# Edge messages of a graph layer on one core: term rows in two float32r parts, and four selected columns instead of three in every other pair

## What is computed

```python
h = relu(layernorm(x))                         # x: 12500 nodes x 32
e_feat = concat([h[src], h[dst], edge_attr])   # 412500 edges, sorted by dst; 32 + 32 + 32 features
v = relu(e_feat @ W1 + b1) @ W2 + b2           # 96 -> 64 -> 32
x_cand = segment_max(v, dst, 12500)            # maximum over the edges of each destination node
out = x + maximum(x_cand, h)
```

## Time and profile before

| what | value |
|---|---|
| median of 3 runs | 3399.03 us (3394.15 to 3399.92) |
| profiled execution, its time | 3395.84 us |
| its span | 3394.0 us |
| PE busy, share of the span | 93% |
| DVE and POOL busy | 75% each |
| ACT (ScalarE) busy | 22% |
| selected columns, gathered columns | 604, 2620 |

### The profile page before, as it was taken

The page is one execution under the profiler, slowest core; times in us unless marked ns, Lnnn a source line. Parts: engine busy times, 40 slices in busy tenths (PEclk is TensorE's granted clock), DMA queues, the critical chain, the costliest instruction groups (busy, mean ns, idle before and its releaser), DMA issues.

```text
span 3394.0 us, 50502 instructions
## 1 busy us (share of the span) xinstructions
PE 3143.3 (93%) x14306; PEld 2377.7 (70%) x14306; DVE 2536.5 (75%) x4366; ACT 748.6 (22%) x1058; POOL 2533.3 (75%) x2651
## 2 busy tenths in 40 slices
PE   2699999999999999999999999999999999999996
PEld 1477777777777777676777777777776777777774
DVE  8387887887887777777777777776777777777776
ACT  5022222222222222222222222222222222222221
POOL 6777777777777777777777777777777777777774
PEclk9799999999999999999999999999999999999998
DMA  5623333333333333333333333333333333333331
GB/s 129 158 70 81 81 80 77 79 79 81 80 77 81 75 78 70 76 73 74 72 74 77 71 76 71 76 76 70 76 73 74 74 74 75 69 78 72 75 70 33
DMA packets 239673, 263.56 MB, mean 78 GB/s; under 512 B 80044, under 2 KB 193310, under 8 KB 233072
## 3 DMA queue, kind: packets, MB, share of 16 engines
q10 hardware_dynamic: 20790, 103.55, 12.3%
q1 hardware_dynamic: 134330, 115.08, 11.2%
q0 software_dynamic: 84352, 43.18, 10.5%
HBM read 250.01 MB, written 11.62 MB: 77 GB/s over the span
## 4 chain that ended last, share of the span: by engine, by line
POOL 46%; PE 29%; issue 15%; DVE 4%; DMA 3%; SPq 2%; POOLq 1%; DVEq 0%; ACT 0%
POOL feat L517 46%; PE ps_spare L608 16%; PE ps_hid L617 3%; PE ps_hid L619 3%; DMA feat<-h_rows,idx 2%; PE ps_picked L649 2%; PE ps_val L628 2%; PE ps_feat L575 1%; SPq L336 1%; PE ps_val L638 1%; DVE feat_t L919 1%; DVE sel_tmp L994 0%; POOLq L505 0%; SPq L303 0%; DVE best L1033 0%
## 5 line engine op out<-in xcount | busy, mean ns | idle before, releaser
L517 POOL DMA_INDIRECT feat<-h_rows,idx x2620 | 2516.5, 960 | 817.4 <-issue 790.2
L608 PE MATMUL ps_spare<-table,key_hot 128*128 128x448 f32 x8456 | 1942.7, 385 | 31.0 <-DVE key_hot L983 25.0
L608 PEld LDWEIGHTS ps_spare<-table,key_hot 128*128 128x128 f32 x8456 | 1616.0, 193 | 266.1 <-issue 127.6
L1033 DVE TENSOR_TENSOR best<-ps_picked,best 32x64 f32 x1612 | 356.1, 221 | 565.9 <-PE ps_picked L649 376.9
L983 DVE TENSOR_TENSOR key_hot<-key_ring,ps_iota 128x896 fp32r<-128x896 f32 x604 | 650.7, 1078 | 30.4 <-DMA key_ring<-key_rows 30.4
L617 PE MATMUL ps_hid<-feat_t,w_blk 128*128 128x512 f32 x806 | 432.7, 618 | 0.0
L994 DVE SCALAR_TENSOR_TENSOR sel_tmp<-off_place,offset,ps_spare 128x448 f32<-128x448 f32 x604 | 407.4, 675 | 12.3 <-PE ps_spare L608 9.3
L619 PE MATMUL ps_hid<-edge_hot,dst_rows 128*128 128x512 f32 x806 | 411.6, 592 | 0.0
L1001 DVE TENSOR_REDUCE feat<-sel_tmp 128x32 f32<-128x448 f32 x604 | 374.5, 620 | 20.8
L758 ACT ACTIVATE hidden<-ps_hid,b_col 128x1024 f32<-128x1024 f32 x202 | 225.4, 1116 | 606.3 <-PE ps_hid L619 606.3
L770 ACT CAST ends<-ps_val 128x512 fp32r<-128x512 f32 x202 | 118.2, 585 | 1020.7 <-PE ps_val L638 1015.7
(11 more groups left out here) (122 smaller groups left out, 770.8 us busy)
## 6 DMA issues: line engine op xcount, KB each, us to landing
dst_rows<-loc_rows ACTq DMA_DIRECT2D x98, 512.0 KB
feat_t<-attr_rows_in ACTq DMA_DIRECT2D x98, 512.0 KB
feat<-h_rows,idx POOLq DMA_INDIRECT x2620
key_ring<-key_rows SPq DMA_DIRECT2D x101, 384.0 KB, 3.4
dst_rows<-term_rows SPq DMA_DIRECT2D x404, 64.0 KB
dst_rows<-keep_rows SPq DMA_DIRECT2D x100, 256.0 KB
term_rows<-best SPq DMA_DIRECT2D x3, 1792.0 KB
idx<-src_cols_in SPq DMA_DIRECT2D x51, 32.0 KB
```

Source lines behind the costliest of these rows:

```text
L517: nc.gpsimd.indirect_dma_start(feat[:, slot, k, :], None, h_dram, bass.IndirectOffsetOnAxis(ap=idx[:, c % IDX, k:k + 1].bitcast(U32), axis=0),
L608: mm = pe.matmul(ps_sel[j % 2], key_hot[:, j % HOTS, g, :], table[half][:, g, :], start=(g == 0 and half == 0), stop=(g == SG - 1 and half ...
L1033: mm = nc.vector.tensor_tensor(col, ps_picked[D * q:D * q + D, to:to + WIN], col, ALU.max)
```

## The change

`SEL` becomes (4, 3): even pairs have 4 selected columns, odd pairs 3. A helper `columns(v)` gives the number of the first column of pair v. The term rows are split as the table already was: ScalarE rounds them into one float32r part, DVE subtracts for the second, and the first layer multiplies each by a one-hot that is now float32r too. `HOTS` goes from 4 to 2.

```diff
-SEL = 3
-HOTS = 4
+SEL = (4, 3)
+SPAN = len(SEL)
+HOTS = 2
...
+def columns(v):
+    return sum(SEL) * (v // SPAN) + sum(SEL[:v % SPAN])
...
-        edge_hot = sb("edge_hot", [P, 2, 4 * P])
+        edge_hot = sb("edge_hot", [P, 2, 4 * P], F32R)
+        term_half = [sb(f"term_half{n}", [P, 2, P], F32R) for n in range(2)]
...
-            sp.wait_ge(S["key_out"], 16 * NSB)
-            sp.wait_ge(S["off_step"], 5)
-            win_dmas(sp.dma_start, x, x_even, False, 0, T, S["x_win_in"])
...
+            sp.wait_ge(S["key_out"], 16 * NSB)
             for n in range(2):
-                load_key(2 * SEL * n, n)
+                load_key(columns(2 * n), n)
...
+            sp.wait_ge(S["sel_ready"], columns(NP - 1) + 1)
+            win_dmas(sp.dma_start, x, x_even, False, 0, T, S["x_win_in"])
             sp.wait_ge(S["best_done"], 1)
...
             def first_layer(i, v):
                 pe.wait_ge(S["edge_hot_ready"], i * UP + v + 1)
+                pe.wait_ge(S["term_split"], i * UP + v + 1)
...
-                    mm = pe.matmul(ps_hid[:, c, :], term_ring[:, slot, :], edge_hot[:, c, :],
-                                   start=False, stop=True, skip_group_check=True)
+                    for half in range(2):
+                        mm = pe.matmul(ps_hid[:, c, :], term_half[half][:, c, :], edge_hot[:, c, :],
+                                       start=False, stop=half == 1, skip_group_check=True)
...
             def step(i, v):
-                ahead = [j for j in range(SEL * v + 2 * SEL - 1, SEL * v + 3 * SEL - 1) if is_column(i, j)]
+                mid = [j for j in range(columns(v + 1) + 2, columns(v + 2)) if is_column(i, j)]
+                ahead = [j for j in range(columns(v + 2), columns(v + 2) + 2) if is_column(i, j)]
...
-                for j in ahead[0:1]:
+                for j in mid[0:1]:
                     select(i, j)
...
+                for j in mid[1:2]:
+                    select(i, j)
                 first_layer(i, v)
-                for j in ahead[1:3]:
+                for j in ahead:
                     select(i, j)
...
+            def round_terms(i, v):
+                n, slot = wide(i, v), TWO * v % RING
+                if v % 2 == 0:
+                    act.wait_ge(s_aux[v // 2 % 2], i * (2 * AUX) + (v // 4 * AUX + AUX))
+                nc.scalar.copy(term_half[0][:, 0:n, :], term_ring[:, slot:slot + n, :]).then_inc(S["term_hi_ready"], 1)
...
+            def split_terms(i, v):
+                n, slot = wide(i, v), TWO * v % RING
+                dve.wait_ge(S["term_hi_ready"], i * UP + v + 1)
+                nc.vector.tensor_tensor(term_half[1][:, 0:n, :], term_ring[:, slot:slot + n, :],
+                                        term_half[0][:, 0:n, :].bitcast(F32), ALU.subtract
+                                        ).then_inc(S["term_split"], 1)
...
                 place_edges(i, v)
+                split_terms(i, v)
                 for j in ahead[0:1]:
                     take_selected(i, j)
```

More of the change, by code:

```diff
@@ L103, in gnn_layer @@
         key_hot = sb("key_hot", [P, HOTS, SG, P], F32R)
-        key_ring = sb("key_ring", [P, 4 * SEL, P])
+        key_ring = sb("key_ring", [P, columns(4), P])
+        falls = sb("falls", [P, CE], BF16)
+        sel_tmp = sb("sel_tmp", [P, SN])
         offset = sb("offset", [P, NSEL])
-        sel_tmp = sb("sel_tmp", [P, SN])
         key_i = sb("key_i", [P, SG], I32)
@@ L254, in gathered @@
         def gathered(c):
-            return COLS - 1 - c % TWO
+            return COLS - (SEL[c // TWO % SPAN] + c % TWO) // TWO
         def is_column(i, j):
-            return not known(i) or j < SEL * (NP - 1) + 1
+            return not known(i) or j < columns(NP - 1) + 1
         def column(j):
-            n = j % SEL
-            return TWO * (j // SEL) + min(n, 1), COLS - 1 - n // 2
+            v = max(v for v in range(NP) if columns(v) <= j)
+            n = j - columns(v)
+            return TWO * v + (0, 1, 1, 0)[n], COLS - 1 - n // 2
         def load_rows(eng, s, half, count):
@@ L351, in load_key @@
             def load_key(s, half):
-                lo, n = half * 2 * SEL, 2 * SEL
+                lo, n = columns(2 * half), columns(2 * half + 2) - columns(2 * half)
                 sp.dma_start(key_ring[:, lo:lo + n, :].rearrange("p c e -> p (c e)"),
@@ L567, in turn_features @@
                 n = wide(i, v)
-                pe.wait_ge(S["sel_ready"], i * (SEL * UP) + (SEL * v + (SEL if n > 1 else 1)))
+                pe.wait_ge(S["sel_ready"], i * columns(UP) + (columns(v + 1) if n > 1 else columns(v) + 1))
                 for c in range(TWO * v, TWO * v + n):
@@ L675, in _ @@
             pe.wait_ge(S["table_ready"], 2)
-            for j in range(2 * SEL - 1):
+            for j in range(columns(1) + 2):
                 select(0, j)
@@ L1039, in step @@
             def step(i, v):
-                ahead = [j for j in range(SEL * v + SEL, SEL * v + 2 * SEL) if is_column(i, j)]
+                ahead = [j for j in range(columns(v + 1), columns(v + 2)) if is_column(i, j)]
                 if later(i, v - 1):
@@ L1052, in step @@
                     keep_best(i, v - 2)
-                for j in ahead[2:3]:
+                for j in ahead[2:]:
                     take_selected(i, j)
@@ L1070, in _ @@
                 place_keys(0, j)
-            for j in range(SEL):
+            for j in range(columns(1)):
                 take_selected(0, j)
@@ L1137 @@
     blocks = [np.asarray(src)[a:a + CE].reshape(2, P, Q)[1] for a in padded[0:len(begins) + len(begins) % 2]]
-    picked = np.stack([block[:, q] for n in range(0, len(blocks), 2)
-                       for block, q in ((blocks[n], Q - 1), (blocks[n + 1], Q - 1), (blocks[n + 1], Q - 2))])
+    picked = np.stack([blocks[TWO * v + (0, 1, 1, 0)[n]][:, Q - 1 - n // 2]
+                       for v in range(len(blocks) // TWO) for n in range(SEL[v % SPAN])])
     given["sel_rows"], given["sel_cols"] = picked, picked.T
```

37 lines of the change are left out of this document (18 added, 19 removed).

## The result

The changed kernel takes 3465.27 us (median of 4 runs, 3463.39 to 3466.4), against 3398.41 for the kernel before in the same series: ratio 1.02, 95% interval 1.0186 to 1.0213. Said was 3432. The direction was right, the size half of what came. The profiled execution took 3465.08, its span is 3463.2.

A forecast was written before the change was run, and what follows sets the result against it. Before, PE and later POOL's gathers bound it; after, a DVE-PE ring at 16.20 us per step. 197 x (16.20 - 15.96) = +47, start -9, end -5: +33 on 3395.84 gives 3429, median 3432; range 3355 to 3510.

The forecast's parts named there:

- The ring: In the loop, DVE and PE wait on each other through the one-hot; sets the step at 16.20 us, +47 in all.
- the end: The three steps behind the 200th: less term work and no gather wait, -5 us.
- the start: Before the third step: keys load earlier because x no longer loads ahead of them, -9 us.
- the walk of the ring: Sum of DVE and PE pieces from one pick_ends: 15.07 us with three takes, 17.32 with four, mean 16.20.
- Restart and select: In the loop, PE restarts after the one-hot, 0.28 us, then does the select's 14 matmuls, 2.82 us.
- steps of alternately about 14.4 and 18 us: Sign in the loop that would show the forecast right: step times alternating between these two lengths.
- PE's own work: PE's matmuls per loop step, without waits: 15.72 us, bounds 15.60 and 16.5.
- float32r term matmul: First-layer term matmul of 512 columns on PE: 0.235 us, bounds 0.206 and 0.43.
- The subtraction: New DVE instruction for the second term part, 256 elements, in the loop: 0.35 us, bounds 0.1 and 0.69.
- Rival 2: In place_edges on DVE, float32r one-hot loses double pace: step 16.66 us, total 3523; chance 0.14, shared with similarly large waits.
- the likeliest case: The loop's DVE and PE cycle as walked, with its bounds: 3406 to 3480 us, chance 0.56.
- The lesser form of rival 2: In the loop, POOL's gathers and the SBUF subtraction delay each other by 0.1 to 0.2: 3450 to 3470, counted with the forecast.

The follow-up runs named there:

- section 5: Series where the kernel before took 4373 to 4452 us instead of 3398: variants in buffers, take order, x load and columns, ratios to it 1.009 to 1.109.

## Why the prediction was right and where it was wrong

- **Who bounds.** Right. The ring closed, and four buffers, which open it and leave the rest, are 115 us faster.
- **The size.** Forecast +33, measured +69.2 us of span: the branch +53.4 that was not in the sum, the rest of the ring 24 us shorter than said, the end 5.4 and the start 1.1 us longer than said.
- **The step that failed** is the walk of the ring: "take 2.25 ... scan 1.13", and from it "Sum 15.07 ... Mean 16.20 us". It took DVE's time from one step in the middle of a turn and held it for all. Every eighth step has the branch between take and scan. The profile of before had the row for it: the scan's idle time, ended by "issue", 23 times. It belongs to the terms that a slack hides, and the change took the slack. It was put at nothing. Measured it is 34.5 us of idle time on DVE, 40 us in the steps and, with the lower clock behind nine of them, +53 us.
- **The rest of the ring** was 0.12 us too long per step (16.08 for 16.20), 24 us in all, which hid nearly half of the miss. Restart and select take 3.00 instead of 3.10, the three-take step 14.95 instead of 15.07; in the step with four takes, 17.20 for 17.32, PE's own 17.12 is as good as the bound. (The sign "steps of alternately about 14.4 and 18 us" does not follow from the prediction's own 15.07 and 17.32, and it was not seen.)
- **PE's own work** 15.675 (said 15.72), and the float32r term matmul at about 0.235 (0.233 from its start to the next matmul's): right. The subtraction 0.34 (said 0.35), `edge_hot` at its old pace:

```profile
L995 DVE TENSOR_SCALAR edge_hot<-dst_rows,place 128x1024 fp32r<-128x1024 bf16 x202 | 151.0, 747 | 4.7 <-DMA dst_rows<-term_rows 4.5
```

  Rival 2 falls with this row: 747 ns, 740 before. That was right for the reason given.
- **Start** -7.9 (said -9): right in size. The cause rests on when the keys were issued (section 5), not on a run with x alone moved in normal conditions.
- **End** +0.4 (said -5). Behind the second layer of the 200th step the changed kernel still has two selects to do, the kernel before one; the next step takes 12.87 us for 10.83. The prediction counted only what becomes cheaper there.
- **GpSimd** waits for engines now, as said: 134.5 us for the scan, and its "issue" waits are 711.4 instead of 790.2 us.
- The sign was right. The time lay in the range and even in the likeliest case's own, 3406 to 3480, but that was luck: these bounds stood for the restart and the subtraction, which came out near the middle, and a term that was in none of them filled the room. The lesser form of rival 2 named 3450 to 3470 for gathers and the subtraction holding each other up. That was not it either: no piece of the ring on DVE is longer than walked, and with four buffers the same work fits into PE's own time.

## What to carry to other kernels

Before a buffer count is halved, walk from the reader of the buffer back to its writer. If the walk returns to the reader, its length is a floor under the step, and it must be walked through every kind of step, the one with the loop's branch first. Look in the waits for idle time ended by "issue" that comes as often as the loop turns: it costs nothing only as long as something slower covers it. If it can't be covered, a long instruction directly ahead of DVE's branch hides part of it, as the one-hot of 1.08 us did here beside the maximum of 0.2.

## What the runs showed of the hardware

- The loop's taken branch stops DVE's sequencer for 2.76 to 3.54 us until the next instruction (23 turns each of two kernels). 1.5 us of it show as idle time behind a one-hot of 1.08 us, 3.3 behind a maximum of 0.2. The 24th branch, which leaves the loop, stops nothing, and in the changed kernel PE and ScalarE pass their taken branches in 0.16 to 0.29 us.
- After PE has waited 2.05 to 2.45 us at such a turn, its granted clock falls to 0.50 (1.2 GHz) in 9 of 23 turns, and the select's 14 matmuls take 4.66 instead of 3.15 us. With four buffers, where that wait for a one-hot is missing, the clock stays at its upper level through the loop. The length of the wait alone does not decide it: the clock fell after waits of 2.05 and 2.29 us and stayed up after 2.22 and 2.45.
